# Count steps in every unit of the self pass, with two alternating sets of loop one-hots

## The chip, the cores and the metric

The kernel runs on one core of a Trainium2 chip. The metric is the device time of one execution in microseconds (us). Engines: PE is TensorE (PEld its weight loads), DVE is VectorE, ACT is ScalarE, POOL is GpSimd, SP the engine that issues most transfers.

## The reference

1250 nodes with 1024 features, 40000 edges sorted by target. Two graph layers, then a spiking feed-forward block:

```
mean = segment_sum(h[src], dst) / max(degree, 1)
h' = h @ W_self + mean @ W_neigh + b      # layer 0 with relu, layer 1 without
x  = x + layer1(layer0(layernorm(x)))
x  = x + rate of 5 spiking steps over (relu(ln(x) @ W_fc)^2 @ W_proj)
```

## The kernel before

Nodes stand in 10 tiles of 128 rows (TILES = 10). The graph part is six passes of 10 units each: A0 (h @ W_neigh0, kept in SBUF as z), S0 (h @ W_self0, the "self pass", stored to DRAM as parts), G0 (the aggregation: adjacency counts times z, plus the part), then A1, S1 and G1 for the second layer. `dense` (L1532) does one unit of A or S: 48 matmuls of 128x512 (8 slices of the contraction, 3 high/low passes, 2 halves), all at L1552. `aggregate` (L1615) does one unit of G: 40 matmuls at L1623, and in layer 0 also a small `degree` product.

**The adjacency.** G0 needs a dense matrix of edge counts, which is made during A0 and S0. Its 80 windows of 16 targets are built one after the other, from window 56 round to 55 (`window_of`). For a window, edges come in chunks of 125; each chunk is a product of two one-hot matrices, source (125x128) and key (125x160), at L1487. The sum of a window lies in PSUM bank 4 or 5, alternately. A window has a head of 2 chunks (`HEAD_CHUNKS`) and then turns of a loop, each with 4 chunks or, in its short form, 2. Most windows have one turn; windows 0 to 9 and 12 have extra ones (`EXTRA_TURNS`; window 0 has 8). A **step** is one turn, with the head if it is the window's first. There are 101 steps, and a step has 4 or 6 products.

**Who makes the one-hots.** POOL makes the source one-hots of the heads (`head_of_block`, L719: a copy at L721, two one-hots at L726), for two windows in turn (sets 0 and 3). DVE makes the keys of the heads (L1121), and for the loop all keys (L1134) and the sources of the loop's first set (L1132), in `key_one_hots` (L1114). ACT makes the sources of the second set in two operations (L829, L834, `src_one_hots`), and copies a finished window out of PSUM (L851, `copy_counts`). The loop has one pair of sets, 1 and 2. So DVE waits on `hot_used` until PE has used the set before it fills it anew, and so does ACT at L834. PE (`step_of_edges`, L1501, `turn_of_edges`, L1490) waits for key and source of each set. POOL waits until PE has used the head two windows back.

**Where the steps are put.** `STEP_SLOTS` (L101) puts steps between the 48 matmuls of a unit: one in A0 unit 3, four each in units 4 to 8 (from slot 12), two in unit 9, three in S0 unit 0 (slots 36, 40 and 44), nine or ten each in S0 units 1 to 8, none in S0 unit 9. The order of work on each engine is written out by hand. In S0 unit p, DVE first takes the sums of unit p-1 out of PSUM (`take_self`, L1241), then makes the one-hots of all steps of the unit but the first, then those of the first step of unit p+1.

**Buffers.** Eight windows make one count tile of 128 targets. Two tiles of SBUF hold the counts; each is stored to DRAM (`store_counts`). They and all one-hots lie where the adjacency tiles `at0` and `at1` are loaded for G0. So the loads of the first two adjacency tiles wait for the last store of counts (SP queue, end of S0). The landing space of W slices 0 and 1 is `w_raw` (8 KB a partition). W_neigh1 is loaded and split into high and low parts (`high_of_w` on ACT, `low_of_w` on DVE) during G0: slices 0 and 1 in units 0 and 1, slice n in unit n from 2 to 7. `rows` are four 4 KB buffers: 0 and 1 for parts, 2 and 3 for LayerNorm and G0's results.

Of the kernel before, what the change touches and what calls it, by code (L numbers as in the profile page):

```python
# [6 lines left out]
F32 = mybir.dt.float32  # L7
# [28 lines left out]
HEAD_SETS, LOOP_SETS = (0, 3), (1, 2)  # L36
SETS = 4
HOT_AT = {0: 0, 3: HEAD_CHUNKS, 1: 2 * HEAD_CHUNKS, 2: 2 * HEAD_CHUNKS + LOOP_SET}
HOTS = 2 * (HEAD_CHUNKS + LOOP_SET)
ACT_SET = 2  # L40
LOOP_CHUNKS = LOOP_SET * len(LOOP_SETS)
# [22 lines left out]
A0_STORES = (7, 9)  # L64
# [45 lines left out]
def steps_of(unit):  # L110
    return [step for _, step in STEP_SLOTS.get(unit, [])]

# [5 lines left out]
def gnn_ffn(nc, x, dst_cols, src_cols, dst_rows, w_self0, w_neigh0, b0, w_self1, w_neigh1, b1,  # L118
            w_fc, w_proj, out):
    with ExitStack() as ctx:  # L120
# [29 lines left out]
        def put_from(address, *what):  # L150
# [43 lines left out]
        at_raw = [tile[:, :, :].bitcast(F32) for tile in at]  # L194
        counts_tile, edge_col, iota, current, src_hot, key_hot = put_from(
# [3 lines left out]
            ("key_hot", [P, HOTS, WINDOW_COLS], BF16))  # L199

# [213 lines left out]
        def w_lows(phase, k):  # L414

            return KD * phase + k + 1
# [60 lines left out]
        def _(sp):  # L477
# [104 lines left out]
            for j in range(2):  # L582
                sp.dma_start(at_raw[j][:, :, :], at_dram[j]).then_inc(at_in[j], 16)
            store_part(S0, TILES - 1)
            load_part(0, 0)
            load_part(0, 1)


            for n in range(TILES):
                if n >= 1 and n + 1 < TILES:  # L590
                    load_at(G0, n + 1)
                if 2 <= n < KD:
                    load_w(2, n)
# [101 lines left out]
        def _(pool):  # L695
# [23 lines left out]
            def head_of_block(pair, side, first, end):  # L719
# [5 lines left out]
                for c in range(HEAD_CHUNKS):  # L725
                    ins = nc.gpsimd.tensor_scalar(src_hot[:, HOT_AT[HEAD_SETS[side]] + c, :], iota[0:P, 0:128],  # L726
# [48 lines left out]
        def _(act):  # L775
# [43 lines left out]
            closed = act.alloc_register("act_closed")  # L819

            def src_one_hots(i, j):

                count = chunks_of_set(i, j)
                first, end = turns_of_step(act, registers, edge, i, j)
                with act.Fori(first, end, count * len(LOOP_SETS)) as g:
                    act.wait_ge(act_hot_ready, visit)
                    for c in range(count):
                        chunk = g + (count * LOOP_SETS.index(ACT_SET) + c)
# [4 lines left out]
                    act.wait_ge(hot_used[ACT_SET], visit)  # L833
                    nc.scalar.activation(src_hot[:, HOT_AT[ACT_SET]:HOT_AT[ACT_SET] + count, :], dist[:, 0:count, :],  # L834
                                         ACT.Relu, bias=1.0, scale=-1.0).then_inc(act_hot_ready, 1)
                    act.reg_add(visit, visit, 1)
                if j == extra_turns(i) > 0:
                    act.reg_mov(closed, visit)

            def copy_counts(i, j):  # L840
# [5 lines left out]
                if extra_turns(i) > 0:  # L846
                    act.wait_ge(hot_used[ACT_SET], closed)
# [59 lines left out]
            for n in range(TILES):  # L907
                if n < 2:
                    high_of_w(2, n)
                if n >= 1:  # L910
                    high_of_row(1, n - 1, ACT.Relu)
                if 2 <= n < KD:
                    high_of_w(2, n)
# [111 lines left out]
        def _(dve):  # L1025
# [82 lines left out]
            visit = dve.alloc_register("dve_visit")  # L1108
            dve.reg_mov(visit, 1)
# [4 lines left out]
            def key_one_hots(i, j):  # L1114
                v = window_of(i)
                if j == 0:
# [3 lines left out]
                    for c in range(HEAD_CHUNKS):  # L1120
                        ins = nc.vector.tensor_scalar(key_hot[:, HOT_AT[s] + c, :], iota[0:P, :], float(v * WINDOW_COLS),  # L1121
                                                      current[:, side, 1, c:c + 1], ALU.add, ALU.is_equal)
                    ins.then_inc(key_hot_ready[s], 1)
                count = chunks_of_set(i, j)
                first, end = turns_of_step(dve, registers, edge, i, j)
                with dve.Fori(first, end, count * len(LOOP_SETS)) as g:
                    for place, s in enumerate(LOOP_SETS):
                        dve.wait_ge(hot_used[s], visit)
                        for c in range(count):
                            chunk = g + (count * place + c)  # L1130
                            if s != ACT_SET:
                                nc.vector.tensor_scalar(src_hot[:, HOT_AT[s] + c, :], iota[0:P, 0:128],  # L1132
                                                        edge_col[:, 0, ds(chunk, 1)], None, ALU.is_equal)
                            ins = nc.vector.tensor_scalar(key_hot[:, HOT_AT[s] + c, :], iota[0:P, :], float(v * WINDOW_COLS),  # L1134
# [50 lines left out]
            def low_of_w(phase, k):  # L1185
                dve.wait_ge(w_high, KD * phase + k + 1)
# [61 lines left out]
            def sum_at(n):  # L1248
# [4 lines left out]
                nc.vector.tensor_reduce(at_sum[:, :], at_raw[n % 2][:, :, :].rearrange("p a d -> p d a"), AX.X,  # L1253
# [24 lines left out]
            for p in range(TILES):  # L1278
# [3 lines left out]
                for step in steps[1 if p else 0:]:  # L1282
                    key_one_hots(*step)
                for step in steps_of(S0 + p + 1)[0:1]:
                    key_one_hots(*step)
            sum_at(0)
            take_self(S0, TILES - 1)


            for n in range(TILES):  # L1290
# [3 lines left out]
                if n < 2:  # L1294
                    low_of_w(2, n)
# [500 lines left out]
```

## Time and profile before

| | us |
|---|---|
| median of 3 runs | 1611.92 (1611.5 to 1613.23) |
| the profiled execution's own time | 1612.89 |
| span of its profile | 1611.1 |
| PE busy | 1584.1 (98%) |
| DVE, ACT, POOL busy | 874.0, 457.9, 142.9 |

In a timeline row the first number is the start in us from the span's start, the second how long the group lasted; "x4" counts its instructions, and brackets say how long the engine idled before it and what ended that. "issue" is idle time for which the profile shows no wait. "SPq" is SP's queue of transfers.

### The profile page before, as it was taken

To read this page: it belongs to the slowest core of one execution; us is meant where nothing else is said; L and a number is where in the kernel's file an instruction comes from. 1 tells how busy PE (TensorE), PEld (TensorE's weight loads), DVE (VectorE), ACT (ScalarE), POOL (GpSimd) and SP (SyncE) were. 2 spreads that over 40 slices of the span, in tenths; PEclk is the share of its full clock that TensorE was granted. 3 is DMA by queue.
4 is the path that set the end of the run, shared out by engine and by line. 5 is a ranking of instruction groups with operands and counts; after the bars stand their busy time and mean duration, and the time that the engine had idled before them with its cause. 6 is when DMAs were issued, how large, how long until landed. Compare 5 with 4: busy or idle time off the path is not lost.

```text
span 1611.1 us, 23194 instructions
## 1 busy us (share of the span) xinstructions
PE 1584.1 (98%) x7728; PEld 1332.8 (83%) x7728; DVE 874.0 (54%) x1643; ACT 457.9 (28%) x857; POOL 142.9 (9%) x279
## 2 busy tenths in 40 slices
PE   7999999999999999999999999999999999999997
PEld 5877666888888888889989899898998888888885
DVE  7776776465113223555334344343443788888878
ACT  3345565121112000114123132130221333333356
POOL 1242368100000000010000000000001000000001
PEclk9999999999999999999999999999999999999999
DMA  8323334575533554568112021130222333333312
GB/s 299 131 96 130 100 112 167 179 271 216 190 104 131 206 193 159 179 200 316 54 53 94 33 82 52 52 104 26 78 74 108 105 117 117 117 117 117 105 65 50
DMA packets 55706, 205.47 MB, mean 128 GB/s; under 512 B 5360, under 2 KB 14078, under 8 KB 50084
## 3 DMA queue, kind: packets, MB, share of 16 engines
q1 hardware_dynamic: 52772, 190.19, 33.3%
q0 software_dynamic: 2848, 14.16, 2.6%
q8 instruction: 52, 0.85, 0.2%
q14 instruction: 34, 0.28, 0.1%
HBM read 153.85 MB, written 52.04 MB: 128 GB/s over the span
## 4 chain that ended last, share of the span: by engine, by line
PE 97%; DVE 1%; issue 1%; DMA 0%; ACT 0%; DVEq 0%; SPq 0%; ACTq 0%; POOL 0%; POOLq 0%
PE bank L1552 27%; PE bank L1674 27%; PE bank L1693 24%; PE bank L1623 11%; PE bank L1731 3%; PE bank L1487 2%; PE bank L1528 2%; PE bank L1750 0%; DMA pr_raw<-w_proj 0%; DMA rows<-x 0%; DVE key_hot L1134 0%; DVE xt L1175 0%; DVE key_hot L1121 0%; DVE src_hot L1132 0%; DVEq L1134 0%
## 5 line engine op out<-in xcount | busy, mean ns | idle before, releaser
L1552 PE MATMUL bank<-w,xt 128*128 128x512 f32 x1920 | 469.3, 397 | 2.8 <-DVE w L1187 2.6
L1674 PE MATMUL bank<-x2t,fc_w 128*128 128x384 f32 (+1 forms) x2304 | 438.4, 350 | 0.8 <-ACT relu L954 0.8
L1674 PEld LDWEIGHTS bank<-x2t,fc_w 128*128 128x128 f32 x2304 | 411.7, 188 | 26.0 <-issue 1.1
L1552 PEld LDWEIGHTS bank<-w,xt 128*128 128x128 f32 x1920 | 354.1, 189 | 74.0 <-issue 3.8
L1693 PE MATMUL bank<-pr_w,hid 128*128 128x512 f32 (+1 forms) x1728 | 394.8, 389 | 0.0
L1693 PEld LDWEIGHTS bank<-pr_w,hid 128*128 128x128 f32 (+1 forms) x1728 | 320.6, 186 | 70.8
L1399 DVE TENSOR_TENSOR y<-y,bank 128x512 f32<-128x512 f32 (+1 forms) x144 | 98.7, 686 | 207.0 <-PE bank L1693 207.0
L1623 PE MATMUL bank<-z,at 128*128 128x512 f32 x800 | 187.1, 392 | 0.0
L1623 PEld LDWEIGHTS bank<-z,at 128*128 128x128 f32 x800 | 148.8, 188 | 30.3
L949 ACT ACTIVATE pr_w<-pr_raw 128x1024 fp32r<-128x1024 f32 x64 | 67.1, 1049 | 365.6 <-PE bank L1693 362.2
L1342 DVE TENSOR_TENSOR square<-relu 128x384 f32<-128x384 f32 (+1 forms) x96 | 56.8, 592 | 144.3 <-ACT relu L954 144.3
L954 ACT ACTIVATE relu<-bank 128x384 f32<-128x384 f32 (+1 forms) x96 | 49.9, 520 | 227.9 <-PE bank L1674 227.9
L726 POOL TENSOR_SCALAR src_hot<-iota,current 125x128 bf16<-125x128 f16 x160 | 103.7, 658 | 16.2 <-POOL current L721 16.2
L1324 DVE TENSOR_TENSOR fc_w<-fc_raw,fc_w 128x1024 fp32r<-128x1024 f32 x64 | 78.2, 1222 | 8.7 <-ACT fc_w L944 7.6
L1336 DVE TENSOR_TENSOR pr_w<-pr_raw,pr_w 128x1024 fp32r<-128x1024 f32 x64 | 78.0, 1218 | 1.7 <-ACT pr_w L949 1.7
L1181 DVE TENSOR_TENSOR z<-bank,z 128x1024 fp32r<-128x1024 f32 x20 | 24.4, 1222 | 93.9 <-ACT z L805 93.9
L1241 DVE TENSOR_TENSOR rows<-bank,bias 128x1024 f32<-128x1024 f32 x20 | 24.5, 1224 | 84.5 <-PE bank L1552 84.3
L944 ACT ACTIVATE fc_w<-fc_raw 128x1024 fp32r<-128x1024 f32 x63 | 65.9, 1046 | 1.0 <-DMA fc_raw<-w_fc 0.8
L1487 PEld LDWEIGHTS bank<-key_hot,src_hot 125*128 125x128 bf16 x446 | 30.2, 97 | 43.0 <-issue 29.6
L1487 PE MATMUL bank<-key_hot,src_hot 125*128 125x160 bf16 x446 | 56.9, 235 | 6.5 <-DVE key_hot L1134 2.7
L1134 DVE TENSOR_SCALAR key_hot<-iota,edge_col 125x160 bf16<-125x160 f16 x286 | 62.9, 265 | 0.2 <-issue 0.2
L1132 DVE TENSOR_SCALAR src_hot<-iota,edge_col 125x128 bf16<-125x128 f16 x143 | 37.5, 262 | 46.2 <-PE bank L1487 44.6
(141 smaller groups left out, 971.7 us busy)
## 6 DMA issues: line engine op xcount, KB each, us to landing
fc_raw<-w_fc SPq DMA_DIRECT2D x64, 512.0 KB, 4.4
pr_raw<-w_proj SPq DMA_DIRECT2D x64, 512.0 KB, 3.5
xt<-xt_dram SPq DMA_DIRECT2D x24, 1024.0 KB, 5.0
xt_dram<-xt SPq DMA_DIRECT2D x18, 1024.0 KB, 4.3
at<-at_dram SPq DMA_DIRECT2D x20, 640.0 KB, 5.2
part_dram<-rows SPq DMA_DIRECT2D x20, 512.0 KB, 4.0
rows<-part_dram SPq DMA_DIRECT2D x20, 512.0 KB, 4.7
rows<-x SPq DMA_DIRECT2D x18, 512.0 KB, 4.8
```

Of the source, the lines that this page charges most:

```text
L726: ins = nc.gpsimd.tensor_scalar(src_hot[:, HOT_AT[HEAD_SETS[side]] + c, :], iota[0:P, 0:128], current[:, side, 0, c:c + 1], None, ALU.is_e ...
L944: nc.scalar.activation(fc_w[:, q, :, HI, :], fc_raw[:, q, :, :], ACT.Copy).then_inc(fc_high, 1)
L949: nc.scalar.activation(pr_of(j)[:, HI, :], pr_raw[:, j % 2, :], ACT.Copy).then_inc(pr_high, 1)
L1134: ins = nc.vector.tensor_scalar(key_hot[:, HOT_AT[s] + c, :], iota[0:P, :], float(v * WINDOW_COLS), edge_col[:, 1, ds(chunk, 1)], ALU.add, ...
L1324: nc.vector.tensor_tensor(fc_w[:, q, :, LO, :], fc_raw[:, q, :, :], fc_w[:, q, :, HI, :].bitcast(F32), ALU.subtract).then_inc(fc_low, 1)
L1336: nc.vector.tensor_tensor(pr_of(j)[:, LO, :], pr_raw[:, j % 2, :], pr_of(j)[:, HI, :].bitcast(F32), ALU.subtract).then_inc(pr_low, 1)
L1399: nc.vector.tensor_tensor(part, part, bank[0:height, 2 * (n % 2) + q, :], ALU.add).then_inc(y_added, 1)
L1487: return nc.tensor.matmul(bank[:, 4 + i % 2, 0:WINDOW_COLS], src_hot[:, HOT_AT[s] + c, :], key_hot[:, HOT_AT[s] + c, :], start=start, stop ...
L1552: ins = nc.tensor.matmul(bank[:, 2 * (u % 2) + q, :], xt[j][:, a, k, :], w[:, k, b, q * HALF:(q + 1) * HALF], start=(k == 0 and m == 0), s ...
L1623: ins = nc.tensor.matmul(bank[:, 2 * (u % 2) + q, :], left[j][:, s, :], right.bitcast(F32) if exact else right, start=(s == 0 and b == HI) ...
L1674: ins = nc.tensor.matmul(bank[:, 4 + (c if g == 0 else j % 2), 0:n], fc_w[:, j % 2, k, a, :], x2t[g][:, k, v, c0:c0 + n], start=(k == 0 an ...
L1693: ins = nc.tensor.matmul(bank[0:height, 2 * (n % 2) + q, :], hid_of(g, j)[:, a, n * T:n * T + height], pr_of(j)[:, v, q * HALF:(q + 1) * H ...
```

## The change

- Steps are spread anew: five in each of A0 units 4 to 8, three in A0 unit 9, three in S0 unit 0 as before, and seven or eight in each of S0 units 1 to 9.
- A second pair of loop sets, 4 and 5, is laid in free bytes of `w_raw`. Steps of S0 alternate between the pairs ("side"); steps of A0 keep the first. Each side has its own visit counters.
- DVE makes the one-hots of two steps of a unit, not one, before it takes the sums of the unit before.
- The adjacency tiles for G0 units 0 and 1 are loaded in S0 unit 8 into other places: over `rows` 2 and 3 (`at_rows`), and into the upper part of `w_raw` (`at_w`). Those for units 2 and 3 go to `at0` and `at1` once all counts are stored, behind the part loads on SP's queue.
- `w_raw` is therefore free later. Slices 0 and 1 of W_neigh1 are loaded and split in G0 units 3 and 4, beside slices 3 and 4, whose places stay.
- `take_self` of the last unit goes ahead of the first `sum_at`. The first `sum_at` and the first `degree` wait until all windows are copied. Counts are stored in A0 after units 6, 7 and 9, not 7 and 9.

```diff
-HEAD_SETS, LOOP_SETS = (0, 3), (1, 2)
+HEAD_SETS, LOOP_SETS = (0, 3), ((1, 2), (4, 5))
-A0_STORES = (7, 9)
+A0_STORES = (6, 7, 9)
+STEPS_AHEAD = 2
+W2_AT = {2: (2,), 3: (0, 3), 4: (1, 4), 5: (5,), 6: (6,), 7: (7,)}
...
-        [(A0 + 3, 1, 30, 12)] + [(A0 + n, 4, 12, 36) for n in range(4, TILES - 1)] + [(A0 + 9, 2, 12, 12), (S0, 3, 36, 12)]
-        + [(S0 + p, 10 if p in (3, 5, 7) else 9, 0, 48) for p in range(1, 9)]):
+        [(A0 + 3, 1, 30, 12)] + [(A0 + n, 5, 12, 36) for n in range(4, TILES - 1)] + [(A0 + 9, 3, 12, 24), (S0, 3, 36, 12)]
+        + [(S0 + p, 7 if p in (4, 6, 8) else 8, 0, 48) for p in range(1, TILES)]):
...
+OWN_STEPS = [step for p in range(TILES) for step in steps_of(S0 + p)]
+SIDE_OF = {step: (k + 1) % 2 for k, step in enumerate(OWN_STEPS)}
...
+        at_rows = at_address(rows_end - 2 * nbytes([T, D], F32), "at_rows", [128, TILES, T], F32R)
+        at_w = at_address(xt_at - nbytes([128, TILES, T], F32R), "at_w", [128, TILES, T], F32R)
...
+        src_more, key_more = put_from(w_end, ("src_more", [P, MORE_HOTS, 128], BF16),
+                                      ("key_more", [P, MORE_HOTS, WINDOW_COLS], BF16))
...
                     if k < 2:
                         sp.wait_ge(w_low, w_lows(phase - 1, k))
+                        if phase == 2:
+                            sp.wait_ge(pair_done, 2 * (G0 + 2))
...
             def load_at(stage, n):
-                sp.wait_ge(pair_done, 2 * (stage + n - 1 if n >= 2 or stage == G0 else G0 + TILES))
-                sp.dma_start(at_raw[n % 2][:, :, :], at_dram[n]).then_inc(at_in[n % 2], 16)
+                if stage == G0 and n < 2:
+                    sp.wait_ge(row_turned, 2 * turned(0, TILES - 1) + 2)
+                    sp.wait_ge(w_low, w_lows(1, 1))
+                    place = (n - tile_of(0)) % TILES
+                    sp.wait_ge(at_stored[place % COUNT_TILES], 16 * (place // COUNT_TILES + 1))
+                elif stage == G0 and n < 4:
+                    for j in range(COUNT_TILES):
+                        sp.wait_ge(at_stored[j], 16 * (TILES // COUNT_TILES))
+                else:
+                    sp.wait_ge(pair_done, 2 * (stage + n - 1 if n >= 2 else G0 + TILES))
+                sp.dma_start(at_raw_of(stage, n), at_dram[n]).then_inc(at_in[n % 2], 16)
...
+                if p == TILES - 2:
+                    load_at(G0, 0)
+                    load_at(G0, 1)
...
-            load_w(2, 0)
-            load_w(2, 1)
-            for j in range(COUNT_TILES):
-                sp.wait_ge(at_stored[j], 16 * (TILES // COUNT_TILES))
-            for j in range(2):
-                sp.dma_start(at_raw[j][:, :, :], at_dram[j]).then_inc(at_in[j], 16)
             store_part(S0, TILES - 1)
             load_part(0, 0)
             load_part(0, 1)
+            load_at(G0, 2)
+            load_at(G0, 3)
...
-                    act.wait_ge(hot_used[ACT_SET], visit)
+                    act.wait_ge(hot_used[act_set], side_visit)
...
-                with dve.Fori(first, end, count * len(LOOP_SETS)) as g:
-                    for place, s in enumerate(LOOP_SETS):
+                with dve.Fori(first, end, 2 * count) as g:
+                    for place, s in enumerate(LOOP_SETS[side]):
                         dve.wait_ge(hot_used[s], visit)
...
-                for step in steps[1 if p else 0:]:
+                for step in steps[STEPS_AHEAD if p else 0:]:
                     key_one_hots(*step)
-                for step in steps_of(S0 + p + 1)[0:1]:
-                    key_one_hots(*step)
+                if p + 1 < TILES:
+                    for step in steps_of(S0 + p + 1)[0:STEPS_AHEAD]:
+                        key_one_hots(*step)
+            take_self(S0, TILES - 1)
             sum_at(0)
-            take_self(S0, TILES - 1)
...
-            def turn_of_edges(i, count, stop=False):
-                for s in LOOP_SETS:
-                    if s == ACT_SET:
+            def turn_of_edges(i, side, count, stop=False):
+                visit = side_visits[side]
+                for place, s in enumerate(LOOP_SETS[side]):
+                    if place == 1:
                         pe.wait_ge(act_hot_ready, next_visit)
                     pe.wait_ge(key_hot_ready[s], visit)
```

## Rows read from the trace of the kernel before

**Rows 1.** The page: the chain that ended last, by engine
```profile
PE 97%; DVE 1%; issue 1%; DMA 0%; ACT 0%; DVEq 0%; SPq 0%; ACTq 0%; POOL 0%; POOLq 0%
```

**Rows 2.** PE timeline, first pass, two steps nine products apart: start us, length us, engine, line
```profile
94.66 0.45 PE L1487 MATMUL bank<-key_hot,src_hot 125*128 125x160 bf16 x4
94.91 2.31 PE L1552 MATMUL bank<-w,xt 128*128 128x512 f32 x9
97.06 0.45 PE L1487 MATMUL bank<-key_hot,src_hot 125*128 125x160 bf16 x4
```

**Rows 3.** PE timeline, end of the self pass
```profile
288.57 12.51 PE L1552 MATMUL bank<-w,xt 128*128 128x512 f32 x54
300.92 6.52 PE L1623 MATMUL bank<-z,at 128*128 128x512 f32 x28
```

**Rows 4.** Source view of L1487, first pass: count, what its engine idled for (us, times)
```profile
L1487 PE MATMUL bank<-key_hot,src_hot x92: 232/233/244, 60.1 to 135.4; 125*128 125x160 bf16 x92
...
  issue: 6.0, 23
```

**Rows 5.** The same for the self pass; the last two are who waited for it
```profile
L1487 PE MATMUL bank<-key_hot,src_hot x354: 229/233/246, 150.6 to 288.5; 125*128 125x160 bf16 x177
...
  issue: 24.9, 92
  DVE key_hot L1134: 10.8, 24
...
  ACT src_hot L834: 41.6, 68
  DVE src_hot L1132: 30.1, 49
```

**Rows 6.** PE timeline, units 4 and 5 of the self pass
```profile
150.56 0.98 PE L1487 MATMUL bank<-key_hot,src_hot 125*128 125x160 bf16 x4
...
223.39 0.59 PE L1487 MATMUL bank<-key_hot,src_hot 125*128 125x160 bf16 x6
223.78 1.17 PE L1552 MATMUL bank<-w,xt 128*128 128x512 f32 x4
225.35 0.23 PE L1487 MATMUL bank<-key_hot,src_hot 125*128 125x160 bf16 x1 [0.40 <-DVE key_hot L1121]
...
226.69 1.40 PE L1552 MATMUL bank<-w,xt 128*128 128x512 f32 x5
```

**Rows 7.** DVE timeline, the same unit boundary
```profile
223.59 1.23 DVE L1241 TENSOR_TENSOR rows<-bank,bias 128x1024 f32<-128x1024 f32 x1 [0.24 <-PE bank L1552]
224.73 0.48 DVE L1121 TENSOR_SCALAR key_hot<-iota,current 125x160 bf16<-125x160 f16 x2
...
226.12 0.42 DVE L1121 TENSOR_SCALAR key_hot<-iota,current 125x160 bf16<-125x160 f16 x2
```

**Rows 8.** ACT timeline, two one-hot sets in the self pass
```profile
236.74 0.69 ACT L829 ACTIVATE dist<-iota,edge_col 125x128 bf16<-125x128 f16 x2 [0.83 <-issue]
...
238.30 0.40 ACT L829 ACTIVATE dist<-iota,edge_col 125x128 bf16<-125x128 f16 x1 [0.23 <-issue]
```

**Rows 9.** POOL timeline, head one-hots in the self pass
```profile
228.85 0.19 POOL L721 COPY current<-edge_col 125x4 f32 x1
...
230.55 0.19 POOL L721 COPY current<-edge_col 125x4 f32 x1
```

**Rows 10.** Timeline, head one-hots on POOL beside LayerNorm on DVE, first pass
```profile
102.89 1.69 POOL L726 TENSOR_SCALAR src_hot<-iota,current 125x128 bf16<-125x128 f16 x2 [0.20 <-POOL current L721]
```

**Rows 11.** Timeline around the start of the first aggregation
```profile
306.48 0.80 SPq L534 DMA_DIRECT2D rows<-part_dram  x2
...
311.61 1.29 DVE L1270 SCALAR_TENSOR_TENSOR rows<-bank,dinv,rows 128x1024 f32<-128x1024 f32 x1 [3.66 <-DMA rows<-part_dram]
```

**Rows 12.** Windows: PE, PEld, DVE, ACT, POOL busy (instructions), PEclk, DMA share, GB/s
```profile
289.00:301.00 12.00, 12.00 (x55) 9.91 (x54) 2.05 (x2) 2.23 (x3) 0.00 (x0) 1.00 0.81 297
...
330.60:340.80 10.20, 10.20 (x52) 8.58 (x51) 6.21 (x8) 2.04 (x3) 0.00 (x0) 1.00 0.72 271
```

More of the change, by code:

```diff
@@ L586, in _ @@
             load_part(0, 1)
+            load_at(G0, 2)
+            load_at(G0, 3)
             for n in range(TILES):
-                if n >= 1 and n + 1 < TILES:
+                if n >= 3 and n + 1 < TILES:
                     load_at(G0, n + 1)
-                if 2 <= n < KD:
-                    load_w(2, n)
+                for k in W2_AT.get(n, ()):
+                    load_w(2, k)
                 if n >= 1:
@@ L819, in _ @@
             closed = act.alloc_register("act_closed")
+            side_visits = [act.alloc_register(f"act_visit{side}") for side in range(2)]
+            for side_visit in side_visits:
+                act.reg_mov(side_visit, 1)
             def src_one_hots(i, j):
                 count = chunks_of_set(i, j)
+                side = side_of(i, j)
+                act_set, side_visit = LOOP_SETS[side][1], side_visits[side]
                 first, end = turns_of_step(act, registers, edge, i, j)
-                with act.Fori(first, end, count * len(LOOP_SETS)) as g:
+                if (i, j) == OWN_STEPS[0]:
+                    act.wait_ge(w_low, w_lows(1, 1))
+                with act.Fori(first, end, 2 * count) as g:
                     act.wait_ge(act_hot_ready, visit)
                     for c in range(count):
-                        chunk = g + (count * LOOP_SETS.index(ACT_SET) + c)
+                        chunk = g + (count + c)
                         ins = nc.scalar.activation(dist[:, c, :], iota[0:P, 0:128], ACT.Square,
@@ L907, in _ @@
             for n in range(TILES):
-                if n < 2:
-                    high_of_w(2, n)
                 if n >= 1:
                     high_of_row(1, n - 1, ACT.Relu)
-                if 2 <= n < KD:
-                    high_of_w(2, n)
+                for k in W2_AT.get(n, ()):
+                    high_of_w(2, k)
             for p in range(TILES):
@@ L1298, in _ @@
                 inverse_degree(n)
-                if 2 <= n < KD:
-                    low_of_w(2, n)
+                for k in W2_AT.get(n, ()):
+                    low_of_w(2, k)
             take_aggregate(0, TILES - 1)
@@ L1495, in turn_of_edges @@
                     for c in range(count):
-                        ins = product_of_chunk(i, s, c, stop=(stop and s == ACT_SET and c == count - 1))
+                        ins = product_of_chunk(i, s, c, stop=(stop and place == 1 and c == count - 1))
                     ins.then_inc(hot_used[s], 1)
@@ L1514, in step_of_edges @@
                 first, end = turns_of_step(pe, registers, edge, i, j)
-                with pe.Fori(first, end, count * len(LOOP_SETS)):
-                    turn_of_edges(i, count, stop=(j == last > 0))
+                with pe.Fori(first, end, 2 * count):
+                    turn_of_edges(i, side_of(i, j), count, stop=(j == last > 0))
                 if last == 0:
@@ L1622, in products @@
                             right = z[:, s, b, q * HALF:(q + 1) * HALF]
-                            ins = nc.tensor.matmul(bank[:, 2 * (u % 2) + q, :], left[j][:, s, :],
+                            own = left[:, s, :]
+                            ins = nc.tensor.matmul(bank[:, 2 * (u % 2) + q, :], own.bitcast(F32) if exact else own,
                                                    right.bitcast(F32) if exact else right,
@@ L1631, in aggregate @@
                     for s in range(TURN_AT):
-                        products(at, s, exact=False)
+                        products(s, exact=False)
                 if l == 0:
```

79 lines of the change are left out of this document (52 added, 27 removed).

## The prediction, made before any run of the changed kernel

> **What bounds the kernel now.** I read the page's chain first: the chain that ended last is PE for 97% of the span [rows 1]. So time is won only where PE idles, or where its own work takes longer than it must. PE's products don't change: the same 101 steps with the same 446 count products (92 in the first pass, 354 in the self pass [rows 4, 5]) and the same dense products. The question is what a step costs PE beyond its own work, and this is read from PE's timeline, pass by pass.
>
> The first pass shows the clean price. Two steps of 4 products lie nine dense products apart and start 2.40 us apart [rows 2]. A dense product alone takes (300.92 - 288.57) / 54 = 0.2287 us [rows 3]. So a clean step of 4 products costs 2.40 - 9 x 0.2287 = 0.34 us. For one of 6, dense work resumes 0.39 us after the first product instead of 0.25 [rows 6, 2], which makes 0.48. All 23 steps of the first pass are clean in this sense, though the source view puts 6.0 us of "issue" idling down to them, 0.26 us each [rows 4]: that much belongs to a clean step.
>
> The self pass is not clean. From its first step at 150.56 to the first aggregation at 300.92 are 150.36 us [rows 6, 3]. In that time lie 480 - 36 = 444 dense products, 101.5 us, and 78 steps with 354 products [rows 5], so 57 steps of 4 and 21 of 6: 57 x 0.34 + 21 x 0.48 = 29.5 us. What is left, 150.4 - 101.5 - 29.5 = 19.4 us, is lost. With 0.345 and 0.485 unrounded it is 19.0, and I take **19.0 us**: all that a better feeding of the steps could bring.
>
> Where it is lost is seen at the unit boundary [rows 6]. The first step of unit 5 starts at 223.39. Clean, the second would start 0.48 + 4 x 0.229 us later, at 224.79, and dense work would resume at 225.18; it resumes at 226.69, so 1.5 us are lost. DVE's timeline says why [rows 7]: at 223.59 it begins to take the last unit's sums (1.23 us), and only then makes the one-hots of the second step. Seven other units repeat this, with 1.0 to 1.6 us each, some 10 us in all. The other 9 us lie in ordinary steps, 0.1 to 0.4 us each. There DVE and ACT wait for PE to have used the one pair of sets, 30.1 us and 41.6 us in all [rows 5], and then PE waits for the refilled set. It is a ping-pong between engines none of which is full.
>
> **The change, part by part.**
>
> *Five steps a unit in the first pass.* Six steps of 0.34 us, 2.1 us, move from the self pass into the first: no change in the sum. They stand seven dense products apart, a pitch of 7 x 0.229 + 0.34 = 1.9 us. What DVE does for a step after its set comes free is three one-hots, some 0.5 us at 1.39 / 8 each [rows 7], and ACT one operation, so this stays hidden. DVE has LayerNorm in the same unit; the next row is needed at slot 6 of the next unit and now comes about 1 us later relative to the unit's start, with about as much to spare. I price it at nothing; if that cover were gone it would cost some tenths in five units, under 2 us. Bounds 0 and +2.
>
> *Two sets by turns.* With a second pair, DVE and ACT may fill the set of step k+2 as soon as PE is done with step k. The pitch of steps becomes 6 x 0.229 + 0.48 = 1.86 us in units of eight steps of 6 products, and 6 x 0.229 + 0.34 = 1.71 us where all have 4. Against this stands the speed of each feeder. DVE, unhindered, needs 1.39 us for a full step (from 224.73 to 226.12 [rows 7]). Eight of them and the 1.23 us of the sums are 12.4 us, in a unit of 11.0 + 8 x 0.48 = 14.9. ACT needs 1.56 us (236.74 to 238.30 [rows 8]) against 1.86. POOL needs 1.70 us from one head to the next (228.85 to 230.55 [rows 9]) against 1.86, and against 1.71 in the light units. All fit, POOL just so, and its buffers let it run about 1.3 us late before PE sees it. So the 9 us of ordinary steps should go nearly whole. Bounds: 9 us, and nothing.
>
> *Two steps ahead of the sums.* After the sums, DVE has to make the third step, which starts 12 dense products and two steps into the unit, 2 x 1.86 = 3.7 us. DVE finishes what is ahead about 0.5 us into the unit, the sums at 1.75 and the third step at 3.1. It arrives 0.6 us early, so the eight losses of the boundaries go. Bounds: 10 us, and nothing.
>
> *Steps in unit 9 of the self pass.* They cost PE nothing new, since they come out of other units. They move the last store of counts from just behind 288.57 [rows 3] to the pass's end. The first two adjacency tiles no longer depend on it: they are loaded a unit earlier, into places that are free. The third tile is needed two units of 40 products, over 18 us, into the aggregation. Its load is now queued behind the last part's store and the loads of parts, which went out 5.6 us after the aggregation's start and landed by 10.7 [rows 3, 11]. It should land by 13 to 15 us. The first part is needed for the row that PE transposes 68 products, 15.6 us, in, so that too has cover; with the sums taken ahead of the adjacency sum it even comes 1 us sooner.
>
> *W slices 0 and 1 later.* Units 3 and 4 of the aggregation get one more load of 512 KB, one more ACT and one more DVE operation. DVE is busy 6.2 of 10.2 us there [rows 12], so 7.4 after. The traffic of 271 GB/s at a share of 0.72 becomes about 322 GB/s at 0.86, somewhat over the busiest row shown (297 at 0.81 [rows 12]). The transfers there have most of a unit to spare. Price 0, bounds 0 and +2.
>
> *The start of the self pass* keeps its loss: DVE comes from splitting W_self0 (not touched) and makes the first step's one-hots when PE is already there. In the first row of [rows 6] four products last 0.98 us, where a clean step has 0.45 [rows 2]; with the 6 operations of the new first step I put it at 0.7. For jitter elsewhere, another 0.8. So 1.5 us of the 19.0 remain.
>
> **Sum.** 19.0 - 1.5 = 17.5 us less. From the span of 1611.1 that makes 1593.6; the profiled execution's own time of 1612.9 is 1.8 us over its span and 1.0 over the median, so I set it off against the median: 1611.9 - 17.5 = **1594.4**.
>
> **One rule against it.** POOL's two head one-hots take 1.69 us beside DVE's LayerNorm [rows 10], while the whole POOL round in the self pass takes 1.70 [rows 9], so its work does stretch beside some DVE work. The Trainium skill (SBUF — State Buffer, "Who interferes with whom") says that DVE and GpSimd share one pair of ports as an exclusive lock, which an instruction of DVE in a two-port mode (tensor_scalar can enter one) holds for its whole length. By that rule a DVE that makes its one-hots in an unbroken run would hold POOL back more than now; it is the third rival below.
>
> **The rivals.**
>
> 1. *The boundary losses stay.* If DVE cannot finish two steps ahead before the sums (a late head from POOL holds it, since its order is fixed), the 10 us of the boundaries remain and only the ordinary steps' 9 are won: 1611.9 - 9 + 0.5 = 1603. For it: everything is in one queue. Against it: 2.5 us of slack in each unit by the sum above.
> 2. *It doesn't do what it says.* The source view puts most of PE's idle time in the self pass down to "issue" (24.9 us against 10.8 behind DVE's keys [rows 5]). If that were PE's own branches and register work, a second set would win nothing: 1611 to 1613. Against it: at 0.26 us per clean step [rows 4] some 20 of the 24.9 belong to the clean price.
> 3. *POOL becomes the bound,* and the time is higher than before. Its place is the 46 windows 10 to 55 in units 3 to 9, one head each. Up to a round of 1.8 us it costs 1 to 4 us in the light units (1598). For a loss of over 0.2% it would have to keep all 19.0 us lost and add 3.2, which is 22.2 / 46 = 0.48 us per step, a round of about 2.2 us. The 1.69 of [rows 10] with the copy's 0.19 [rows 9] and the 0.20 between them [rows 10] make 2.1. That slow form is seen only beside LayerNorm, which the self pass has not. At a round of 2.3 the time would be near 1617.
>
> **How the numbers follow.** The forecast has 0.66; rival 1 has 0.14, rival 2 0.06, rival 3 in its mild form 0.08, in its bad form 0.06. The measurement can tell 0.2% (3.2 us) from no change. Faster: 0.66 + 0.14 + 0.08 = 0.88; the same 0.06; slower 0.06. If all stalls go the time is 1592.9, less some tenths of run-to-run spread, so the low end is 1592. The high end takes in rival 1: 1603. This leaves out a little of the forecast's own case, half of rival 1, and rivals 2 and 3 bad, together about 0.2.
>
> **What would show it.** Right: in the self pass the time from the first step to the aggregation, less its dense products, falls from 48.8 us to about 29 us; the second and third steps of each unit resume dense work 0.25 or 0.39 us after their first product; PE's idle time behind DVE's keys falls from 10.8 to under 2 us; there is no PE idle time in the aggregation. Rival 1: the stall moves from the second to the third step of each unit. Rival 2: DVE's and ACT's waits for PE shrink, yet dense work resumes as late as now. Rival 3: POOL has no idle time left in units 5 to 9 and its two one-hots last over 1.5 us. A PE wait for an adjacency tile or for a row in the aggregation would show a term that I priced at nothing.

## The result and the profile after

| | before | after |
|---|---|---|
| median, 4 runs each | 1612.38 (1611.5 to 1613.23) | 1594.92 (1594.28 to 1595.74) |
| span of the profile | 1611.1 | 1593.2 |
| self pass, first count step to the aggregation | 150.56 to 300.92 | 152.71 to 283.37 |

The changed kernel takes 0.9893 of the time before, with a 95% interval of 0.988 to 0.9905: 17.5 us less. The whole of it lies ahead of the first aggregation, which starts 17.55 us earlier. From its start to the first dense product of pass A1 both kernels take 100.87 us.

The page of the kernel after: busy time by engine, and the chain that ended last [rows 1]. PE stays the bound. With the same products its busy time is 11.5 us less. A dense product is on record as 397 ns long in the mean, while the next one starts 0.229 us behind it; so by an estimate from these two the first 0.17 us of a wait count as busy.
```profile
PE 1572.6 (99%) x7728; PEld 1331.6 (84%) x7728; DVE 874.8 (55%) x1643; ACT 462.9 (29%) x857; POOL 140.9 (9%) x279
PE 97%; DVE 1%; DMA 1%; issue 0%; ACT 0%; SPq 0%; ACTq 0%; DVEq 0%
```

The source view of the count products after, self pass (L1543 is the old L1487), which answers to [rows 5]:
```profile
L1543 PE MATMUL bank<-key_hot,src_hot x216: 232/233/246, 154.4 to 281.9; 125*128 125x160 bf16 x108
...
L1543 PE MATMUL bank<-key_more,src_more x112: 230/233/246, 152.7 to 280.1; 125*128 125x160 bf16 x112
its engine sat idle before it (us, times) until:
  issue: 19.8, 75
  DVE key_more L1188: 0.5, 1
  ACT src_hot L884: 0.3, 1
who waited for it (us, times):
...
  DVE src_more L1186: 5.6, 7
  DVE src_hot L1186: 1.9, 6
```
PE's idle time behind DVE's keys is down from 10.8 us (and 1.4 behind those of the heads, L1121) to 0.5. DVE waited 30.1 us for used sets and now waits 7.5; ACT's 41.6 us at its set are gone from the list. What is called "issue" is 19.8 us, and 72 clean steps at the first pass's 0.26 us each make 18.7.

PE's timeline after, a unit boundary of the self pass, here between units 4 and 5 again [rows 6]:
```profile
213.23 0.24 PE L1543 MATMUL bank<-key_hot,src_hot 125*128 125x160 bf16 x1
...
213.61 1.64 PE L1609 MATMUL bank<-w,xt 128*128 128x512 f32 x6
215.09 0.59 PE L1543 MATMUL bank<-key_hot,src_hot 125*128 125x160 bf16 x6
215.48 1.64 PE L1609 MATMUL bank<-w,xt 128*128 128x512 f32 x6
216.96 0.24 PE L1543 MATMUL bank<-key_hot,src_hot 125*128 125x160 bf16 x1
```
The steps start at 213.23, 215.09 and 216.96, a pitch of 1.86 us, which is 6 dense products and a clean step. Nothing is lost at the second step or at the third.

DVE's timeline at the same place [rows 7], and POOL's [rows 9]:
```profile
213.54 1.21 DVE L1295 TENSOR_TENSOR rows<-bank,bias 128x1024 f32<-128x1024 f32 x1
214.68 0.42 DVE L1171 TENSOR_SCALAR key_hot<-iota,current 125x160 bf16<-125x160 f16 x2
...
216.07 0.43 DVE L1171 TENSOR_SCALAR key_hot<-iota,current 125x160 bf16<-125x160 f16 x2
```
```profile
213.99 0.19 POOL L764 COPY current<-edge_col 125x4 f32 x1 [0.36 <-PE bank L1543]
214.38 1.26 POOL L769 TENSOR_SCALAR src_hot<-iota,current 125x128 bf16<-125x128 f16 x2 [0.20 <-POOL current L764]
215.85 0.19 POOL L764 COPY current<-edge_col 125x4 f32 x1 [0.21 <-PE bank L1543]
```
DVE takes the sums at 213.54, 0.3 us into the unit, and from 214.68 makes the one-hots of the third step. It is done with them by 216.07, when it turns to the fourth; PE gets to the third at 216.96. POOL waits 0.2 to 0.4 us for PE in each of these rounds: it keeps up, with little to spare.

The end of the pass and the aggregation after, PE and then SP's queue and DVE [rows 3, 11]:
```profile
283.37 6.52 PE L1684 MATMUL bank<-z,at_rows 128*128 128x512 f32 x28
```
```profile
288.38 0.86 SPq L582 DMA_DIRECT2D at<-at_dram  x2
...
292.92 1.28 DVE L1326 SCALAR_TENSOR_TENSOR rows<-bank,dinv,rows 128x1024 f32<-128x1024 f32 x1 [2.52 <-PE bank L1684]
```
The third and fourth adjacency tile are asked for 5.0 us into the aggregation. DVE's first aggregate now waits for PE's own products and no longer for a part.

Windows of units 3 and 4 of the aggregation after, where a W slice was added (columns as in [rows 12]):
```profile
313.20:323.40 10.20, 10.20 (x52) 8.59 (x51) 6.21 (x8) 2.98 (x4) 0.00 (x0) 1.00 0.86 324
323.40:333.50 10.10, 10.10 (x51) 8.49 (x51) 7.26 (x9) 2.98 (x4) 0.00 (x0) 1.00 0.87 320
```

### The profile page after: what moved, and what is told of

It is laid out like the page before. It is cut to its first block, busy times and chain, and to the rows that moved or that the text cites. A ratio compares the mean times of both kernels' runs of the same rounds, so it can differ in the third digit from the quotient of the medians.

```text
span 1593.2 us, 23208 instructions
## 1 busy us (share of the span) xinstructions
PE 1572.6 (99%) x7728; PEld 1331.6 (84%) x7728; DVE 874.8 (55%) x1643; ACT 462.9 (29%) x857; POOL 140.9 (9%) x279
## 4 chain that ended last, share of the span: by engine, by line
PE 97%; DVE 1%; DMA 1%; issue 0%; ACT 0%; SPq 0%; ACTq 0%; DVEq 0%
PE bank L1609 27%; PE bank L1735 27%; PE bank L1754 25%; PE bank L1684 11%; PE bank L1792 3%; PE bank L1543 2%; PE bank L1585 2%; PE bank L1811 0%; DVE w L1241 0%; DMA w_landing<-w_self 0%; DMA pr_raw<-w_proj 0%; DMA rows<-x 0%; DVE stats L1196 0%; DVE xt L1229 0%; DVE rows L1212 0%
## 5 line engine op out<-in xcount | busy, mean ns | idle before, releaser
L1684 PE MATMUL bank<-z,at 128*128 128x512 f32 x720 | 168.4, 392 | 0.0
L1684 PEld LDWEIGHTS bank<-z,at 128*128 128x128 f32 x720 | 133.9, 188 | 27.2
L823 ACT ACTIVATE std<-mean_var,eps_col 128x1 f32<-128x1 f32 x20 | 5.9, 295 | 190.5 <-DVE mean_var L1199 190.5
L840 ACT ACTIVATE xt<-bank 128x512 fp32r<-128x512 f32 x48 | 26.2, 596 | 115.5 <-PE bank L1585 115.5
L879 ACT ACTIVATE dist<-iota,edge_col 125x128 bf16<-125x128 f16 x143 | 52.9, 398 | 18.2 <-issue 13.8
L1401 DVE TENSOR_TENSOR hid<-square,hid 128x384 fp32r<-128x384 f32 (+1 forms) x92 | 54.2, 589 | 4.0 <-DVE square L1397 0.3
```

Of the source, the lines that this page charges most:

```text
L1401: nc.vector.tensor_tensor(hid[:, LO, c0:c0 + n], square[:, slot, 0:n], hid[:, HI, c0:c0 + n].bitcast(F32), ALU.subtract).then_inc(hid_low, 1)
L1684: ins = nc.tensor.matmul(bank[:, 2 * (u % 2) + q, :], own.bitcast(F32) if exact else own, right.bitcast(F32) if exact else right, start=(s ...
```

## The experiments

**The measure.** For every count step I take, from the start times of PE's products, the time from the last dense product ahead of it to the first behind it, less 0.229 us, less the clean step's 0.25 (4 products) or 0.39 (6). That is what the step lost. These sums are worked out from the traces of all kernels in the same way, one profiled execution each. Over the 101 steps the kernel before lost 18.9 us and the kernel after 1.7 us. The forecast had 19.0 and 1.5.

Three things may have brought this: the new places of the steps ("new" or "old" slots), the second pair of sets, and two steps ahead of the sums. Seven further kernels and the one after fill all eight combinations. The one with old slots, one pair and one step ahead has everything else of the change: the other places of the adjacency tiles, the later W slices, the order at the aggregation.

The edits, each to the changed kernel, alone or together. The last one gives the slots of before, with the stores of counts that belong to them:
```diff
-STEPS_AHEAD = 2
+STEPS_AHEAD = 1
...
-    return SIDE_OF.get((i, j), 0)
+    return 0
...
-        [(A0 + 3, 1, 30, 12)] + [(A0 + n, 5, 12, 36) for n in range(4, TILES - 1)] + [(A0 + 9, 3, 12, 24), (S0, 3, 36, 12)]
-        + [(S0 + p, 7 if p in (4, 6, 8) else 8, 0, 48) for p in range(1, TILES)]):
+        [(A0 + 3, 1, 30, 12)] + [(A0 + n, 4, 12, 36) for n in range(4, TILES - 1)] + [(A0 + 9, 2, 12, 12), (S0, 3, 36, 12)]
+        + [(S0 + p, 10 if p in (3, 5, 7) else 9, 0, 48) for p in range(1, 9)]):
```

*Old slots, one pair, one step ahead.*

> The changed kernel with the old slots, the old pair of sets alone and one step ahead: what is left of the change is the other places of the first adjacency tiles, W slices 0 and 1 made later, and the order at the end of the self pass. I priced these at nothing: within 0.1% of the kernel before, 1611 to 1614, with all 19 us of losses in the same steps and no idle time of PE in the aggregation. Rival (they bring or cost something by themselves): over 3 us away from the kernel before.

Measured: 1612.34 us, ratio to before 1.0002 (0.9992 to 1.0011); 18.4 us lost. The rest of the change costs and brings nothing.

*Old slots, one pair, two steps ahead.*

> Old slots, one pair, two steps ahead of the sums. From the run with the new slots (1598.3), where the second step made ahead was worth 6 us by itself although I had expected nothing of it. If the order of the sums is a gain of its own, of the 10 us of the boundaries about half go here and the 9 us of ordinary steps stay: 1605 to 1608. If it needs the wide pitch (PE's first use frees the set early enough only with 6 dense products between), the loss moves to the third step whole: 1611 to 1613.

Measured: 1607.56 us, 0.997 (0.9959 to 0.9981). The second steps of the units lose 1.8 us instead of 10.0, the third steps 4.5 instead of 1.3.

*Old slots, two pairs, one step ahead.*

> Old slots, two pairs, one step ahead. With the new slots the second pair brought 1 us here, since all that was left stood at the unit boundaries. With the old slots the 9 us of ordinary steps are there to be won, less what POOL takes (6 us in the run with two steps ahead, part of which it makes good during the boundary stalls): 1604 to 1607, with 8 to 10 us at the second steps. Rival (sets are worth nothing without the step ahead): 1611 to 1613.

Measured: 1607.96 us, 0.9971 (0.9961 to 0.998), 1 us over the expectation. The second steps keep 9.9 us; the steps that are neither second nor third fall from 6.4 to 2.5.

*Old slots, two pairs, two steps ahead.*

> The changed kernel with the steps where the kernel before had them (nine or ten a unit, none in the last unit of the self pass), but two pairs of sets and two steps ahead. My theory: PE's clean pitch falls to 5.1 x 0.229 + 0.48 = 1.65 us (1.51 for 4 products), below POOL's 1.70 us per head, so POOL becomes the bound in units 4 to 8: 46 heads x 1.70 = 78 us against 72.5 us clean, 5 to 6 us lost: about 1600. POOL has no idle time there, and DVE waits for its copy. Rival (POOL doesn't bind and the spreading was not needed): 1594 to 1595.

Measured: 1599.93 us, 0.9922 (0.9905 to 0.9939). 6.8 us are lost, 6.0 of them in units 5 to 8.

*New slots, one pair, one step ahead.*

> The changed kernel with its new slots only: all steps on the one old pair of sets, one step made ahead of the sums. My theory: the wider pitch (6 dense products instead of 5) hides some of the refilling, so of the 9 us of ordinary losses about 3 remain; at each unit boundary the second step is 0.2 us later than before but still made behind the sums, so of 10 us about 5.5 remain. With the 1.5 us of the changed kernel: about 1602 to 1604. Rival A (the second pair is what matters): about 1611, like the kernel before. Rival B (the pitch alone does it all): 1595 to 1597.

Measured: 1604.27 us, 0.9949 (0.9933 to 0.9966); 10.6 us lost. The time is near the expected one, but the split is not: 7.6 us are lost at second steps, where 5.5 were expected, 0.3 at third steps, and 1.3 at all others but those of unit 0 (1.4), where about 3 were expected to remain.

*New slots, two pairs, one step ahead.*

> The changed kernel, with two pairs of sets, but only one step made ahead of the sums. My theory: ordinary steps stay clean; at each of nine unit boundaries the second step's one-hots come 0.2 + 1.23 + up to 1.39 = 2.8 us into the unit, where PE wants them from 1.7 to 1.9 us on, 0.3 to 0.7 us lost each, 4 to 5 us in all: 1599 to 1600. The loss must show at the second step of each unit and nowhere else. Rival (the second pair alone makes the boundary harmless, since keys of both sets can be filled at once): within 1 us of 1594.9.

Measured: 1603.39 us, 0.9944 (0.9928 to 0.9961). The loss sits where it was expected, at the second step of each of the nine units, but with 0.6 to 1.0 us each, 7.6 in all, where 4 to 5 had been expected. DVE's and PE's timelines of this kernel show why:
```profile
217.63 1.23 DVE L1295 TENSOR_TENSOR rows<-bank,bias 128x1024 f32<-128x1024 f32 x1 [1.49 <-PE bank L1609]
218.77 0.48 DVE L1171 TENSOR_SCALAR key_hot<-iota,current 125x160 bf16<-125x160 f16 x2
...
219.65 0.59 DVE L1188 TENSOR_SCALAR key_hot<-iota,edge_col 125x160 bf16<-125x160 f16 x3
```
```profile
219.40 0.23 PE L1543 MATMUL bank<-key_hot,src_hot 125*128 125x160 bf16 x1
220.03 0.84 PE L1543 MATMUL bank<-key_hot,src_hot 125*128 125x160 bf16 x5 [0.40 <-DVE key_hot L1188]
```
DVE has nothing to do for 1.49 us, because next in its order are sums that PE has not finished. It then makes the second step's sets too late for 219.40. A free set cannot help: the order holds DVE back, not the set.

*New slots, one pair, two steps ahead.*

> The changed kernel with all steps on one pair of sets, two steps ahead of the sums. My theory: the second step ahead cannot be filled before PE has used the first of the unit, so DVE takes the sums only some 1.8 us into the unit and the third step is late by some 0.7 us; ordinary steps lose some 3 us in all: 1601 to 1604, no better than with one step ahead, and the loss sits at the third step. Rival (the order of the sums is what counts, not the pair): 1596 to 1598.

Measured: 1598.27 us, 0.9912 (0.9895 to 0.9928). The expectation of 1601 to 1604 was wrong. With six dense products between two steps, a set is free soon enough after its use: second steps lose 0.3 us, the steps that are neither second nor third 1.1. The third steps lose 2.4, one of them at 220.35:
```profile
220.35 0.64 PE L1543 MATMUL bank<-key_hot,src_hot 125*128 125x160 bf16 x3
221.25 0.48 PE L1543 MATMUL bank<-key_hot,src_hot 125*128 125x160 bf16 x3 [0.26 <-DVE key_hot L1188]
```

**The eight together.** Medians, and in brackets the us lost by the measure above:

| | old, pair 1 | old, pair 2 | new, pair 1 | new, pair 2 |
|---|---|---|---|---|
| ahead 1 | 1612.3 (18.4) | 1608.0 (14.5) | 1604.3 (10.6) | 1603.4 (9.5) |
| ahead 2 | 1607.6 (14.8) | 1599.9 (6.8) | 1598.3 (5.1) | 1594.9 (1.7) |

A median less its loss lies between 1592.8 and 1594.0 in all eight, while the medians are 17 us apart: the measure accounts for the time. The new slots are worth 4.6 to 9.3 us, the order 4.8 to 8.5, and the second pair 0.9 to 7.6 (the 0.9 is within the spread of its runs). The terms are not independent: the pair is worth 7.6 with old slots and two ahead, and 3.4 in the kernel after.

**Is POOL the next bound?** With old slots, both other parts in, 6.8 us are still lost. Units 1 to 4 are clean. In the first three at most half of the steps need a head, since their windows have extra turns. In unit 4 eight of nine do, but most have 6 products, and clean they lie 1.70 us apart. From unit 5 on every step has one. POOL's timeline there:
```profile
245.83 0.19 POOL L764 COPY current<-edge_col 125x4 f32 x1
246.22 1.18 POOL L769 TENSOR_SCALAR src_hot<-iota,current 125x128 bf16<-125x128 f16 x2 [0.20 <-POOL current L764]
247.34 0.19 POOL L764 COPY current<-edge_col 125x4 f32 x1
247.73 1.48 POOL L769 TENSOR_SCALAR src_hot<-iota,current 125x128 bf16<-125x128 f16 x2 [0.20 <-POOL current L764]
249.17 0.18 POOL L764 COPY current<-edge_col 125x4 f32 x1
```
It goes from head to head without a pause, in 1.5 to 1.8 us. Of the 40 rounds from 205 to 275 us, 31 are without a wait for PE, and these take 1.62 us in the mean. Clean steps would need a head each 1.44 us (ten a unit, 4 products) to 1.58 (ten a unit, 6 products); the nine of 4 products in units 6 and 8 lie 1.56 apart. Taking work from it is a test: DVE makes the second of the two head sources.
```diff
-                for c in range(HEAD_CHUNKS):
+                for c in range(HEAD_CHUNKS - 1):
...
+                    nc.vector.tensor_scalar(src_of(s, HEAD_CHUNKS - 1), iota[0:P, 0:128],
+                                            current[:, side, 0, HEAD_CHUNKS - 1:HEAD_CHUNKS], None, ALU.is_equal)
```

> Old slots, two pairs, two steps ahead (1599.9 before this edit), but DVE makes one of the two source one-hots of each head, so that POOL's round falls from 1.70 to about 1.1 us and DVE's full step rises by 0.17 to 1.56 us. My theory (POOL bound the light units with the old slots): the 5.9 us lost in units 5 to 8 go, 1594 to 1595.5. Rival (DVE is the bound, by its ten steps and the sums: 10 x 1.39 + 1.23 = 15.1 us in a unit of 15.6): it gets slower, over 1600.

Measured: 1597.22 us, 0.991 (0.9894 to 0.9927), 2.7 us less than without the edit, but 1.7 over the upper end of what was expected. The windows of 205 to 275 us, without the edit and with it (columns as in [rows 12]):
```profile
205.00:275.00 70.00, 68.51 (x401) 47.99 (x401) 53.69 (x245) 44.58 (x137) 58.85 (x123) 1.00 0.44 157
```
```profile
205.00:275.00 70.00, 68.79 (x417) 49.80 (x416) 58.24 (x287) 44.50 (x137) 35.07 (x82) 1.00 0.45 164
```
POOL falls from 58.85 us to 35.07, and the lost time from 6.8 us to 3.4. Of these, 2.5 lie in three single steps. The one that loses 0.91, at 215.76, is the third of unit 5, which has ten steps, most of them with 6 products. DVE comes from the sums there, has one more one-hot to make for each head, and PE waits for its key:
```profile
216.27 0.73 PE L1545 MATMUL bank<-key_more,src_more 125*128 125x160 bf16 x4 [0.27 <-DVE key_more L1190]
```
So the rival of the expectation, DVE, is real in that one place. For the other two (1.0 at 263.62, 0.57 at 248.09) see the last section.

The other way: one more one-hot of 80 columns for POOL in each round, in the kernel after.
```diff
+                nc.gpsimd.tensor_scalar(spare_hot[:, :], iota[0:P, 0:80], current[:, side, 0, 0:1], None, ALU.is_equal)
```

> The changed kernel with one more operation for POOL in each head round, of 80 columns into a place that nobody reads. It should take 0.4 to 0.65 us (the ones of 128 columns take 0.65), so that the round is 2.1 to 2.35 us. My theory (POOL's round is off PE's path as long as it is below the pitch of the steps, and bounds it above): windows 10 to 55 in the self pass take POOL 46 x 2.1 = 97 us at the least, against about 83 us clean for PE, so 10 to 20 us lost in units 3 to 9: 1605 to 1615, the third rival of the prediction made real. Rival (the buffers hide it): below 1598.

Measured: 1603.87 us, 0.9948 (0.9931 to 0.9964), just under the range expected. The mechanism is the expected one, as POOL's timeline shows:
```profile
247.42 0.18 POOL L765 COPY current<-edge_col 125x4 f32 x1
247.81 0.51 POOL L769 TENSOR_SCALAR spare_hot<-iota,current 125x80 bf16<-125x80 f16 x1 [0.20 <-POOL current L765]
248.30 1.22 POOL L771 TENSOR_SCALAR src_hot<-iota,current 125x128 bf16<-125x128 f16 x2
249.47 0.18 POOL L765 COPY current<-edge_col 125x4 f32 x1
```
A round is 2.06 us, and 9.1 us are lost in units 4 to 9. Clean steps lie 1.86 us apart where eight a unit have 6 products (unit 5), and 6 x 0.229 + 0.34 = 1.71 where they have 4, as most here (unit 7). With its two one-hots a round of the kernel after takes 1.60 to 1.66 us at 270 us (0.19 for the copy, 0.20 between, 1.21 to 1.27 for the two). So the kernel after has some 0.2 us of a POOL round to spare in unit 5, and no more than 0.05 to 0.1 in units 7 and 9. A further 1.65 us are lost at the pass's first step (0.7 without the edit). There DVE comes to it at 153.19 and not at 151.89, since it ends the work ahead of it later.

**The loss left at the start.** PE's timeline of the kernel after, the first step of the self pass:
```profile
152.71 0.73 PE L1543 MATMUL bank<-key_more,src_more 125*128 125x160 bf16 x4
153.38 1.18 PE L1609 MATMUL bank<-w,xt 128*128 128x512 f32 x4
```
Dense work resumes 0.67 us after the first product instead of 0.25, and the step itself starts late; 0.7 us are lost in all. The test puts only two steps into unit 0, from slot 40 on, and one more into unit 4.
```diff
-(S0, 3, 36, 12)]
-        + [(S0 + p, 7 if p in (4, 6, 8) else 8, 0, 48)
+(S0, 2, 40, 8)]
+        + [(S0 + p, 7 if p in (6, 8) else 8, 0, 48)
```

> The changed kernel with two steps in unit 0 of the self pass (slots 40 and 44) instead of three (from slot 36), and eight in unit 4. The one large loss that the changed kernel has left, 0.7 us at its first step at slot 36, comes 0.9 us too early for DVE; it should go, and unit 4 with eight full steps should stay clean: 0.7 us less, 1594.2, which the trace shows and the time can't tell. If the loss moves with the step (DVE makes its one-hots only when PE is there), it stays at 0.7.

Measured: 1594.03 us, 0.9887 (0.9871 to 0.9904). The same place in PE's timeline:
```profile
153.34 0.45 PE L1543 MATMUL bank<-key_more,src_more 125*128 125x160 bf16 x4
153.59 1.18 PE L1609 MATMUL bank<-w,xt 128*128 128x512 f32 x4
```
The 0.7 us are gone, and 0.9 us are lost in all instead of 1.7. Unit 4 stays clean with its eight steps. The median is 0.9 us lower, which these few runs cannot tell from no change.

*The same, with POOL relieved as above.*

> The edit before, and DVE makes one of POOL's two source one-hots of each head (which took the loss of the old slots in the light units from 5.9 to 3 us). With the new slots only 0.7 us of small losses are left in units 6 to 9. If they are POOL's, the sum over all steps falls below 0.5 us and the time is 1593.5 to 1594.5; if they are gaps in an engine's own instruction stream, some tenths stay. No difference to the changed kernel that the time can tell.

Measured: 1594.45 us, 0.9891 (0.9874 to 0.9907). The time is as expected, the sum over the steps is not: 1.4 us are lost, where it should have been under 0.5 if the small losses were POOL's. One step of the first pass loses 0.34, and one of unit 7, at 246.29, loses 0.79; all others in units 6 to 9 together lose 0.1. At 246.29 PE waits for DVE, and DVE's timeline has the reason:
```profile
246.30 0.25 DVE L1188 TENSOR_SCALAR src_more<-iota,edge_col 125x128 bf16<-125x128 f16 x1 [1.93 <-issue]
```
A register load of DVE, from 243.76 to 245.62, ends in this gap (see the last section). Relieving POOL wins no time at this pitch. No kernel tried is measurably better than the change itself.

## Why the prediction was right, and where its steps were not

The forecast was 1594.4 us, the result 1594.9. Point by point:

- **What is lost.** 19.0 us were read from two passes of the same kernel, and all steps, taken one by one, lost 18.9. From the first step to the aggregation, less the dense products, it is now 130.66 - 101.5 = 29.1 us; about 29 was forecast.
- **The boundaries,** "some 10 us in all": 9.7 us at the second steps, and 0.1 now. Seven units lose 1.0 to 1.6 us there, and one of the eight, unit 6, only 0.5. Rival 1 did not come, since DVE reaches the sums 0.3 us into the unit. The time that it was given, 1603, is that of the new slots with one step ahead (1603.4 and 1604.3), where the boundary losses do stay.
- **"So the 9 us of ordinary steps should go nearly whole."** They did, but this is the step that failed: it gave them to the second pair alone and priced the new places of the steps at nothing beyond moved work. With one pair and one step ahead, the new slots alone bring 8.1 us, and the losses at steps that are neither second nor third fall from 6.4 to 1.3 us. With 11.0 / 8 us of dense work between steps instead of 11.0 / 9 or less, the ping-pong over one pair mostly fits. In the kernel after the pair is worth 3.4 us, most of it at the third steps, where DVE comes from the sums. The sum came out right because it counted what is lost, whoever wins it back.
- **The start and the jitter,** 0.7 and 0.8 us: 0.71 at the first step, 0.34 at one at 231.8, 0.13 to 0.14 at three more, together with crumbs 1.7. The 0.7 had a mechanism behind it, and it held. The 0.8 had none, so that it came out is luck; the last section shows what stands ahead of these four steps.
- **Priced at nothing.** First-pass steps: no loss over any of them. Aggregation: its length is unchanged. Its windows show 324 and 320 GB/s at a share of 0.86 and 0.87, where 322 at 0.86 was estimated, and DVE at 7.26 us in the second of them where 7.4 was. In the first DVE stays at 6.21, since it begins that unit's second low part only at 323.50. The third adjacency tile is asked for at 288.38 and takes 8.0 us to land in the median of the two: 13 us into the aggregation, PE needs it after 19.
- **Rival 2** is out: what was put down to "issue" is 19.8 us now, nearly all of it the clean steps' own, and the second pair and the order did shorten the pass.
- **Rival 3.** Its mild case is real as a limit (of the 6.8 us lost with old slots and both other parts, half went when POOL was relieved), and the new slots avoid it. Its bad case did not come. POOL's group of head one-hots from 170 to 283 us, before and after:
```profile
L726 POOL TENSOR_SCALAR src_hot<-iota,current 125x128 bf16<-125x128 f16 x99 | 63.8, 655 | 9.9 <-POOL current L721 9.9
```
```profile
L769 POOL TENSOR_SCALAR src_hot<-iota,current 125x128 bf16<-125x128 f16 x102 | 64.7, 644 | 10.3 <-POOL current L764 10.3
```
They average 655 and 644 ns. (By the prediction's own price, a round of 2.2 us costs 3.2 us net, and one of 2.3 another 46 x 0.1; that is near 1620 and not 1617. Neither came.)

DVE's one-hots do lengthen POOL's, though, before as after. In the self pass before, the 10 of POOL's that meet none of DVE's take 597 to 606 ns, and the 100 that meet one take 658 in the mean and up to 800. After, 5 take 594 to 601, and 101 take 650 and up to 781. That is some 50 ns, and the change adds nothing to it. Beside LayerNorm it is another matter. The 1.69 us of [rows 10] are two one-hots of 0.60 and 1.12 us (source view, window 102.8 to 104.6), and the long one begins 0.16 us after LayerNorm's normalising operation on DVE (timeline):
```profile
L726 POOL TENSOR_SCALAR src_hot<-iota,current x2: 602/858/1115, 102.9 to 103.5; 125x128 bf16<-125x128 f16 x2
```
```profile
103.30 0.81 DVE L1158 TENSOR_SCALAR rows<-rows,mean_var,rstd 128x1024 f32<-128x1024 f32 x1
```
In the kernel before, five one-hots begin while that operation runs, and they take 1.03 to 1.21 us; the five that begin ahead of it take 0.60. In the kernel after, where the steps of the first pass stand elsewhere, one begins while it runs (1.03), and four ahead of it (0.60). The rule of the Trainium skill (SBUF — State Buffer, "Who interferes with whom"), by which a DVE instruction in a two-port mode holds the ports that it shares with GpSimd for its whole length, fits these long one-hots, and it does not fit the 50 ns beside DVE's one-hots. In which mode either operation ran, no run here shows.

## What to carry to other kernels

Measure a clean form of the work in the same trace and subtract it from the disputed stretch; that gave the whole gain to 0.1 us, some of it by luck (the jitter). It does not say which edit brings it. When three edits act on one handover between engines (how often it is needed, how many buffers it has, what stands ahead of it in the queue), each is worth little or much depending on the others, so price each with the others absent as well as present. A second buffer does not help where an engine's order holds it at something that is not ready; after it and the order are put right, the next feeder's round time against the pitch (here POOL's 1.6 to 1.7 us against 1.71 to 1.86) is what to look at.

## What was not expected

Each engine loads the bounds of the windows' loops from SBUF into registers, once for two windows (L481). The source view of the kernel after, with min, median and max in ns:
```profile
...
L481 DVEq TENSOR_LOAD <-window_range x40: 340/345/1439, 52.7 to 277.4; - x40
L481 PEldq TENSOR_LOAD <-window_range x40: 327/332/1287, 56.0 to 278.9; - x40
```
The medians are 0.31 to 0.35 us, the longest on each engine 0.9 to 1.4. In the run with the old slots and POOL relieved, one on PE takes 1.83 us, from 262.47 on (source view, then PE's timeline):
```profile
L481 PEldq TENSOR_LOAD <-window_range x1: 1828/1828/1828, 262.5 to 262.5; - x1
```
```profile
263.62 0.24 PE L1545 MATMUL bank<-key_hot,src_hot 125*128 125x160 bf16 x1
264.45 0.36 PE L1545 MATMUL bank<-key_more,src_more 125*128 125x160 bf16 x2 [0.59 <-issue]
```
PE's loop products start when the load has ended (264.30), and this one step loses 1.0 us. At 248.09 a load of 1.19 us on PE ends at 248.35, and the step loses 0.57. These two, and the late step at 215.76, make up 2.5 of the 3.4 us lost in that run.

The same loads stand ahead of what the kernel after still loses. From 150 us on, five of PE's take over 0.7 us. One, at 202.56, ends 1.4 us ahead of the next step and costs nothing. The other four end at 231.84, 246.72, 261.38 and 272.75, at most 0.35 us ahead of their step's first product or behind it, and these are the four steps of 0.34, 0.14, 0.14 and 0.13 us. In the run with the late first step it is the same: its four losses of 0.10 to 0.21 us stand right behind four loads of 0.8 to 1.3 us on PE. No run took a load away, so this is what the traces show and not a test. What makes single loads slow stays open.

The label "issue" also hid more than expected. With old slots, two pairs and two steps ahead, PE's idle time before count products is put down as 26.0 us of "issue" and 1.4 us of all else, although 6.8 us of it are lost time and POOL's rounds cause a good part of it. The clean price per step, not the label, tells the two apart.
